# Query halves through the tail of a Mamba-2 scan block, and a new order of work at the ends of two attentions

## What is computed

```python
# layer 0: cross attention with a mask per sequence, 16 heads of 16, then LayerNorm
Q, K, V = x @ Wq.T + bq, ctx @ Wk.T + bk, ctx @ Wv.T + bv
p = softmax(where(mask == 0, -1e9, Q @ K.T / sqrt(16)))
x = layernorm((p @ V) @ Wo.T + bo + x) * ln_g + ln_b
# layer 1a: a Mamba-2 block
zxbcdt = rms(x) * norm_w @ in_proj_w            # z | xBC | dt
xh, B, C = silu(causal_conv4(xBC))
h_t = h_{t-1} * exp(dt * A) + dt * xh_t * B_t   # 8 heads of 64, state 128
u = rms((h_t . C_t + D * xh) * silu(z)) * gnorm_w
x = x + u @ out_proj_w
# layer 1b: cross attention, 8 heads of 32, mask of the keys
q = layernorm(x) @ Wq
x = x + softmax(where(pad, -1e9, q @ k.T / sqrt(32))) @ v @ Wo
```

## Time and profile before

| what | value |
|---|---|
| median of 3 runs | 8527.78 us (8526.52 to 8528.01) |
| the profiled execution | 8529.28 us |
| its span, first to last instruction | 8527.6 us |
| mean granted TensorE clock | 0.933 of full speed |
| TensorE matmul, busy | 7657.0 us, 90% |
| VectorE, busy | 5273.6 us, 62% |
| ScalarE, busy | 3407.2 us, 40% |
| GpSimd, busy | 1913.5 us, 22% |

### The profile page before, as it was taken

The page is one execution under the profiler, slowest core; times in us unless marked ns, Lnnn a source line. Parts: engine busy times, 40 slices in busy tenths (PEclk is TensorE's granted clock), DMA queues, the critical chain, the costliest instruction groups (busy, mean ns, idle before and its releaser), DMA issues.

```text
span 8527.6 us, 129102 instructions
## 1 busy us (share of the span) xinstructions
PE 7657.0 (90%) x37476; PEld 3496.5 (41%) x37796; DVE 5273.6 (62%) x12605; ACT 3407.2 (40%) x4278; POOL 1913.5 (22%) x1864
## 2 busy tenths in 40 slices
PE   3989999998998989989899899989989899898998
PEld 0353433435334353443534334343343534435343
DVE  3666565765666666666665666656666666666656
ACT  0524435343352434535244352443524345252443
POOL 3040130402203031130401304022030311304113
PEclk6989999899998989999899998999989999998999
DMA  3142230423314132231422304233141332314223
GB/s 73 28 80 38 42 68 10 80 38 51 58 23 75 30 63 55 36 55 28 77 41 37 67 15 80 38 49 60 21 77 31 59 53 34 62 30 73 45 36 63
DMA packets 230684, 422.55 MB, mean 50 GB/s; under 512 B 37209, under 2 KB 128251, under 8 KB 229769
## 3 DMA queue, kind: packets, MB, share of 16 engines
q1 hardware_dynamic: 227927, 413.21, 28.2%
q10 hardware_dynamic: 2048, 0.53, 0.0%
HBM read 191.17 MB, written 8.54 MB: 23 GB/s over the span
## 4 chain that ended last, share of the span: by engine, by line
PE 69%; DVE 12%; issue 8%; ACT 4%; DMA 3%; SPq 2%; POOL 1%; DVEq 1%; ACTq 0%; POOLq 0%
PE ps L1049 12%; PE ps L976 11%; PE ps L938 8%; PE ps L1019 7%; PE ps L1022 6%; DVE mx L1667 5%; PE ps L1024 3%; PE ps L1054 3%; ACT PR L1438 2%; PE ps L1205 2%; PE ps L996 2%; PE ps L1168 2%; PE ps L1259 1%; DVE ps L1702 1%; DMA qst<-qhl 1%
## 5 line engine op out<-in xcount | busy, mean ns | idle before, releaser
L1438 ACT ACTIVATE PR<-ps 128x1024 f32<-128x1024 f32 x2496 | 2503.4, 1024 | 2472.8 <-PE ps L1022 1247.0
L1638 DVE CUSTOM_DVE_ANT_0 ps<-ps,maskq 128x402 f32<-128x402 f32 x4203 | 2410.6, 588 | 1519.8 <-PE ps L976 1372.9
L1049 PE MATMUL ps<-PR,vbuf 128*32 128x512 f32 x9984 | 1343.2, 610 | 29.0 <-ACT PR L1438 24.0
L976 PE MATMUL ps<-kst,qst 96*128 96x402 bf16 (+1 forms) x3115 | 1017.9, 340 | 104.9 <-DVE mx L1638 73.0
L1667 DVE TENSOR_REDUCE mx<-ps 128x2 f32<-128x804 f32 x1024 | 934.1, 988 | 193.8 <-PE ps L996 192.1
L1022 PE MATMUL ps<-maskk,identb 128*128 128x512 bf16 x2592 | 984.9, 380 | 0.0
L1019 PE MATMUL ps<-qst,kst 99*128 99x512 bf16 x2496 | 916.8, 381 | 12.5 <-ACT PR L1438 5.2
L996 PE MATMUL ps<-kst,qst 100*128 100x402 f32 x2048 | 744.1, 489 | 163.6 <-DVE mx L1667 104.8
L1024 PE MATMUL ps<-qst,kst 102*128 102x512 f32 x1664 | 768.0, 526 | 100.3 <-ACT PR L1438 70.9
L976 PEld LDWEIGHTS ps<-kst,qst 96*128 96x128 bf16 x3115 | 281.8, 97 | 1194.4 <-DVE mx L1638 825.5
L756 POOL MEMSET kst<- 96x252 f32 (+1 forms) x34 | 8.7, 256 | 3023.7 <-PE ps L1049 2975.7
(11 more groups left out here) (200 smaller groups left out, 8127.0 us busy)
## 6 DMA issues: line engine op xcount, KB each, us to landing
kst<-khl SPq DMA_DIRECT2D x300, 200.1 KB, 7.5
stage<-in_maskt SPq DMA_DIRECT2D x204, 256.0 KB
stage<-in_mask SPq DMA_DIRECT2D x204, 201.0 KB
kst<-khl SPq DMA_DIRECT2D x96, 402.0 KB, 8.6
kst<-khl SPq DMA_DIRECT2D x96, 398.5 KB, 11.6
ctxs<-in_ctxt SPq DMA_DIRECT2D x17, 1601.0 KB, 17.5
qst<-q1hl SPq DMA_DIRECT2D x96, 256.0 KB
win_s<-in_w_in SPq DMA_DIRECT2D x16, 1288.0 KB, 5.8
```

The source lines that it names most:

```text
L976: pe.matmul(ps[:, bank, 0:w], QS[gi][0:KROWS, h, i * P:(i + 1) * P], KS[gi][0:KROWS, h, c0:c0 + w], start=True, stop=True).then_inc(s_raw, 1)
L1049: mm = pe.matmul(ps[32 * j:32 * j + 32, 6, :], l, PR[:, t % 2, j, :], start=(t == 0), stop=(t == KT - 1), tile_position=(0, 32 * j))
L1438: nc.scalar.activation(PR[:, t % 2, 2 * half:2 * half + 2, :], ps[:, bank:bank + 2, :], ACT.Exp, scale=scale).then_inc(s_p, 1)
L1638: nc.vector.tensor_tensor_reduce(src, src, maskq[:, i, c0:c0 + w], 1.0, -3.0e38, ALU.add, ALU.max, mx[:, c, h * QT + i:h * QT + i + 1]).th ...
```

## The change

Four edits, which touch all engines' programs.

1. *Tail by halves of 256 query rows.* `block_out(0)` and `block_out(1)` move into the scan loop's chunks 2 and 3, `rows_out(0)` to the end of chunk 2. GpSimd's inverse deviations go tile by tile. TensorE's transposes of tiles 0 and 1 stand between the last chunk's transposes and its `wout_s` products; then come the queries of the first half, the transposes of tiles 2 and 3, and the queries of the second half, each half in banks of its own. Copies and low parts go by halves, and twelve transfers of half the size replace the six. The raw pairs take the first half's rows first, head group by head group, and wait for the second half's transfers only at pair 16. TensorE waits for all four low parts before the first pair, as before.
2. *No products of constants*: `idle` is gone.
3. *End of the first attention.* `project_out` of tile 0, first three head groups, stands in front of the last group's last `times_v`, tile 1 ahead of `sums`, tile 2 ahead of `spread`, tile 3 behind it.
4. *End of the second attention.* The output projection goes to banks 4 to 7; tile 3, whose bank the spread uses, comes last as a whole. The wait for `s_fin` moves from the loop's top to behind the first step's scores, and the raw entries of the first group start at step 1 in place of 0.

```diff
-               [(FIRST1 + 48, FIRST1 + 110, 0, KT - 1)], [(FIRST1 + 110, FIRST1 + 160, 1, KT - 1)], \
+               [(FIRST1 + 48, FIRST1 + 110, 1, KT - 1)], [(FIRST1 + 110, FIRST1 + 160, 1, KT - 1)], \
...
         def raw1_place(k):
-            h, i, c = k // (QT * NC // 2), k // (NC // 2) % QT, k % (NC // 2)
+            part, k = k // (UNITS // NHALF), k % (UNITS // NHALF)
+            h, i, c = k // (HT * NC // 2), part * HT + k // (NC // 2) % HT, k % (NC // 2)
...
-        XT1_BANK = [2, 4]
+        XT1_BANK = [4, 2]
+        Q1_BANK = [[5, 7], [0, 1]]
+        NHALF = 2
+        HW = T // NHALF
+        HT = QT // NHALF
...
-            def stack_q1(b, g):
-                sp.wait_ge(s_q1, b * DT + g + 1)
+            def stack_q1(b, part, g):
+                sp.wait_ge(s_q1, (b * NHALF + part) * DT + g + 1)
                 alone(sp)
+                cols1 = slice(part * HW, (part + 1) * HW)
                 for n, (kpart, qpart) in enumerate(TERMS1):
-                    sp.dma_start(f(QS1[g][HD1 * n:HD1 * (n + 1), :, :]), f(q1hl[:, g, qpart, :])).then_inc(s_qs1[g], 16)
+                    sp.dma_start(f(QS1[g][HD1 * n:HD1 * (n + 1), :, cols1]), f(q1hl[:, g, qpart, cols1]))\
+                        .then_inc(s_qs1[g][part], 16)
...
+                if kind == "raw" and k == UNITS // NHALF:
+                    pe.wait_ge(s_qs1[g][1], LEAD + (b + 1) * STACKQ1[1])
...
+                    if gi == 0 and t == 0:
+                        pe.wait_ge(s_fin, LEAD + b * QT)
...
+                    if gi == G0 - 1 and t == KT:
+                        pe.wait_ge(s_norm, LEAD + b * NG + G0 - 1)
+                        pe.wait_ge(s_p, (b * NG + G0) * KT * 2 - 1)
+                        project_out(wo0_s, 0, G0 - 1, G0, range(1))
...
                 for g in range(G0):
                     group(b, g)
+                project_out(wo0_s, 0, G0 - 1, G0, range(1, 2))
                 sums(b, G0 - 1)
...
-                project_out(wo0_s, 0, G0 - 1, G0, range(1))
+                project_out(wo0_s, 0, G0 - 1, G0, range(2, 3))
                 spread(b, G0 - 1)
-                project_out(wo0_s, 0, G0 - 1, G0, range(1, QT))
+                project_out(wo0_s, 0, G0 - 1, G0, range(3, QT))
...
-                project_block(QT - 1)
-
-                def idle(n, bank):
...
-                idle(14, 6)
...
+                project_block(QT - 1, lambda: transposes1(0))
+                queries1(0)
                 pe.wait_ge(s_tj, (b + 1) * (QT - 1))
...
+                transposes1(1)
+                queries1(1)
...
-                pe.wait_ge(s_q1, (b + 1) * DT)
+                pe.wait_ge(s_q1, (b + 1) * DT * NHALF)
...
+                for e in LAST1:
+                    left(b + 1, e)
+                project_out(wo1_s, 0, G1 - 1, G1, range(1), 4)
                 spread(b, NG - 1)
-                project_out(wo1_s, 0, G1 - 1, G1, range(1, QT))
+                pe.wait_ge(s_ctxn, LEAD + b * NG + NG)
+                project_out(wo1_s, 0, G1 - 1, G1, range(1, QT - 1), 4)
                 pe.wait_ge(s_norm, LEAD + b * NG + NG)
-                project_out(wo1_s, G1 - 1, G1, G1)
+                project_out(wo1_s, G1 - 1, G1, G1, range(QT - 1), 4)
+                project_out(wo1_s, 0, G1, G1, range(QT - 1, QT), 4)
...
+                        if c > 1:
+                            block_out(c - 2)
                         dve.wait_ge(s_yp, LEAD + nb + 1)
...
+                            if c == 2:
+                                rows_out(0)
+
+                rows_out(1)
+                block_out(2)
+                block_out(3)
+                rows_out(2)
                 for item in LASTQ:
-                    low_q1(b, item)
+                    low_q1(b, 0, item)
+                rows_out(3)
+                for item in LASTQ:
+                    low_q1(b, 1, item)
```

More of the change, by code:

```diff
@@ L273, in xattn_mamba @@
         s_k1 = [[sem(f"s_k1_{g}_{e}") for e in range(2)] for g in range(G1)]
-        s_qs1 = [sem(f"s_qs1_{g}") for g in range(G1)]
+        s_qs1 = [[sem(f"s_qs1_{g}_{p}") for p in range(2)] for g in range(G1)]
+        s_qp1 = sem("s_qp1")
         s_r1 = sem("s_r1")
@@ L404, in xattn_mamba @@
             pj_bank[item] = 6 + n % 2
-        for n, item in enumerate(LASTQ):
-            pj_bank[item] = n % 2
         ENTRIES = []
@@ L656, in _ @@
                 rows_q1(b)
-                for g in range(G1):
-                    stack_q1(b, g)
+                for part in range(NHALF):
+                    for g in range(G1):
+                        stack_q1(b, part, g)
                 load_pieces(b, bn, PIECE1, QT * NC, False)
@@ L1082, in spread, with project_out @@
                 mm.then_inc(s_spread, 1)
+            def project_out(wo, lo, hi, n, tiles=range(QT), first=0):
+                for i in tiles:
+                    for g in range(lo, hi):
+                        mm = pe.matmul(ps[:, first + i, 0:D], ctxn[:, g, i * P:(i + 1) * P], wo[:, g, :],
+                                       start=(g == 0), stop=(g == n - 1))
+                    if hi == n:
+                        mm.then_inc(s_o, 1)
             def group(b, gi):
@@ L1150, in _ @@
                 second = list(SECOND)
-                def project_q1(item, lo, hi):
-                    i = item[2]
-                    for k in range(DT):
-                        mm = pe.matmul(ps[:, pj_bank[item], lo:hi], wq1_s[:, k, i * P:(i + 1) * P], xn[:, k, lo:hi],
-                                       start=(k == 0), stop=(k == DT - 1))
-                    return mm
                 def fill(n):
@@ L1250, in project_block @@
                     mm.then_inc(s_gt, 1)
+                    if beside_copy is not None:
+                        beside_copy()
                     pe.wait_ge(s_ut, b * QT + c + 1)
@@ L1311, in _ @@
-                idle(3, 1)
-                for i in range(QT):
-                    pe.wait_ge(s_xs1, b * QT + i + 1)
-                    for k in range(DT):
-                        mm = pe.transpose(ps[:, XT1_BANK[k], i * P:(i + 1) * P], xs1[:, i, k * P:(k + 1) * P], ident[:, :])
-                    if i >= QT - 2:
-                        mm.then_inc(s_xst1, 1)
-                    if i == QT - 2:
-                        idle(3, 1)
-                        pe.wait_ge(s_xn1, 2 * DT * b + DT)
-                        for item in LASTQ:
-                            project_q1(item, 0, i * P + P)
@@ L1323, in _ @@
-                pe.wait_ge(s_xn1, 2 * DT * (b + 1))
-                for item in LASTQ:
-                    project_q1(item, (QT - 1) * P, T).then_inc(s_proj, 1)
-                idle(14, 6)
+                transposes1(1)
+                queries1(1)
                 front = list(FRONT)
@@ L1828, in masked_windows, with block_out, rows_out @@
                                             ALU.mult).then_inc(s_M, 1)
+                def block_out(i):
+                    n = b * QT + i + 1
+                    dve.wait_ge(s_op, n)
+                    dve.wait_ge(s_gr, n)
+                    nc.vector.scalar_tensor_tensor(out=xres[:, i, :], in0=ps[:, OUT_BANK[i], 0:D], scalar=rstd[:, 2, i:i + 1],
+                                                   in1=xres[:, i, :], op0=ALU.mult, op1=ALU.add).then_inc(s_blk, 1)
+                    dve.wait_ge(s_blk, n)
+                    nc.vector.bn_stats(stats[:, i, :], xres[:, i, :]).then_inc(s_st1, 1)
+                    dve.wait_ge(s_st1, n)
+                    alone(dve)
+                    nc.vector.bn_aggr(moments[:, i, :], stats[:, i, :]).then_inc(s_mom1, 1)
+                def rows_out(i):
+                    dve.wait_ge(s_rstd1, b * QT + i + 1)
+                    dve.wait_ge(s_mom1, b * QT + i + 1)
+                    nc.vector.tensor_scalar(xs1[:, i, :], xres[:, i, :], moments[:, i, 0:1], rstd[:, 0, i:i + 1],
+                                            ALU.subtract, ALU.mult).then_inc(s_xs1, 1)
                 dve.wait_ge(s_G, b + 1)
```

107 lines of the change are left out of this document (44 added, 63 removed).

## The result

The kernel after takes 8317.3 us (median of 4 runs, 8313.7 to 8325.3), the kernel before 8527.2 (median of 4, 8522.9 to 8528.0): ratio 0.9756, 95% interval 0.9739 to 0.9773, 210 us less. Forecast were 8302 and a range of 8258 to 8385.

What follows compares the result with a forecast made beforehand. TensorE, busy 90% of 8527.6 us, was taken as the bound, so edits pay where it stands still or works ahead of something late. 16 x 10.0 + 16 x 3.7 + 15 x 0.4 = 225 us gave 8303, stated 8302; range 8258 to 8385.

Steps and rivals of the forecast that it cites:

- The tail: Last wout_s group to first raw pair: pair starts at 1054.3, not 1065.0; 10.7 us, less 0.7 for the clock: 10.0.
- first queries: Tail: query products of the first half run from 1046.0 to 1048.0, 2.0 us.
- last rows: Tail: VectorE's rows_out(3), queued behind low parts, ends at 1049.55, +3.5 us from the last wout_s group.
- second queries: Tail: query products of the second half end at 1053.1, +7.0 us from the last wout_s group.
- The transfers: Tail: halves move at 120 GB/s after 2.3 us fixed; the three needed land at 1053.8, before the low parts at 1054.2.
- The first rival: Tail: a half transfer takes as long as a whole; tail loses 1.0 us, total 8479; chance 0.15 including partial cases.
- The clock in the tail: Without constants, TensorE's gaps in the tail lower its clock: 0.7 us lost; nothing counted in the raw stage.
- the second rival: Raw stage: clock stays at half throughout, 16.8 us lost a pass including the tail's 2.2; total 8560; chance 0.03.
- The end of the first attention: Projections fill the 1.34 us hole; VectorE's first add at 1464.0, not 1467.68: 3.7 us a pass, bounds 2.5 to 4.2.
- The end of the second attention: Moved wait worth nothing; raw entries from step 1 remove a 0.48 us wait: 0.4 us, bounds -0.5 and 1.
- The scan: Scan loop: the moved block_outs, some 1.15 us each, fit VectorE's 1.93 us idle and cost nothing.
- Given back behind the raw stage: Second attention's start: GpSimd's chain ends 10.1 us earlier, so nothing is given back; 1.6 us if its waits do not close.

Runs made afterwards that it cites:

- the whole transfers: Kernel after, with six whole q1 transfers, each sent when both halves of its head group are there, in place of twelve halves: 8440.8 us, ratio 0.9901.
- the one without any: Kernel after with first group's raw entries from step 0, wait for s_fin at the loop's top and eight constant products back in the tail: 8256.2 us, ratio 0.9682.

## Why the prediction was right, step by step

- **The tail, 10.0 us a pass: 9.84.** The mechanism, no transfer left in the chain, is shown by the chain and by the whole transfers. The steps from the last `wout_s` group on came at +1.7 (first queries, forecast 2.0), +3.1 (last rows, 3.5), +6.7 (second queries, 7.0), +8.17 (first pair, 8.2).
- **The transfers, 120 GB/s for halves: cautious.** Transfers in 1041 to 1045 us, where these are nearly all that moves (it answers to the earlier trace rows):

```profile
DMA packets 624, 0.56 MB, mean 141 GB/s; under 512 B 73, under 2 KB 624, under 8 KB 624
```

  GpSimd gets the first mask piece 16.0 us behind the last `wout_s` group, not 18.0. The Trainium skill ("DMA: Bandwidth & Descriptors", section Bandwidth) has small transfers far slower than large ones, but in a table of copies from HBM; its part on small descriptors says that transfers within SBUF do not suffer so. This case agrees: 141 GB/s in transfers of 128 KB, 124 in those of 256 KB. The first rival falls with that.
- **The clock in the tail, 0.7 us: mis-sized and put in the wrong place.** It costs 1.5 us in 9 of 16 tails, 0.9 on the mean, but in the other passes it is paid in the raw stage, where I had counted nothing. Putting the constants back is worth 34 us in this kernel. Taking them out of the kernel before cost it 33 by the median, and nothing in the execution with a trace, where scan and first attention made it good. The rule that I cited for the second rival ("TensorE: Matmul & The Clock Gate", Part 1, in the Trainium skill: an array that idles falls to the lower clock) is borne out in that filling the gaps brought 2 us a pass, not as the 16.8 of that rival: from 1046 to 1050 the clock is 0.50, from 1050 to 1060 it is 0.80.
- **The end of the first attention, 3.7: 3.25, and 3.0 when it stands alone.** The hole is filled as forecast. The pass I had read was one of the 13 at the lower clock; three others, with the same gaps, ran at the full clock and had only 1.9 to give. So my reading that gaps of 1.34 and 0.72 us suffice for half speed holds for most passes, not for all. And tile 0 is 0.15 us longer than its hole.
- **The end of the second attention, +0.4: the step that failed.** That the wait's place is worth nothing was right: the jump still takes 3.5 us. The moved entries were forecast to save a wait of 0.48 us; they shortened step 0 by 1.6 us and lengthened the 12 others by 2.8. The first group lost 1.2 us a pass, and with entries from step 0 it got 1.7 back.
- **The scan, 0: +1.6, which is luck.** At a clock of 1.00 it takes 25.8 us in both kernels: the `block_out`s in it cost nothing, as forecast. The gain is the clock's. Before, the scan took 27.5 to 27.6 us at a mean clock of 0.93 to 0.94 in 15 of 16 passes; after, it did so (27.7) in one. The windows of the low stretch in the second pass before, and of a stretch at about the same place after, where the clock was 1.00 all through the scan:

```profile
1015.00:1022.00 7.00, 6.22 (x19) 3.61 (x19) 3.80 (x5) 0.72 (x2) 2.95 (x3) 0.52 1.03 157
```
```profile
1000.00:1007.00 7.00, 5.05 (x39) 4.05 (x36) 5.08 (x7) 1.21 (x3) 1.96 (x1) 1.00 1.04 123
```

  Single edits do this too: without the constants alone the kernel before has one such scan in 16, with the new end of the first attention alone five. So it follows from the edits, by way of the clock, and no term of the prediction held it. It outweighs what the first group lost.
- **Given back behind the raw stage: nothing**, as forecast. GpSimd's last khl part (row L750 at 1085.66) is 52.9 us behind the last `wout_s` group, before 62.5, and 19.98 us ahead of the attention in both.

Forecast were 14.1 us a pass, in terms of 10.0, 3.7 and 0.4; it came to 13.0, as 9.84 + 3.25 - 1.3 + 1.6 - 0.8 and 0.4 of small ones. The total is off by 15 us only because the scan's 1.6 a pass stands against the others' shortfall of some 3.

## What to carry to other kernels

Where a transfer stands in a chain, cut it so that the first consumer needs only its first half; it was the largest part of this gain. Entries spread over steps have to be weighed against the engine that takes them up: freeing one step fills the others. Count a hole before filling it, in recorded instructions, and fill it just short of its end: with constants in the raw stage, 13 more products in the last wait brought the kernel to 5 us below the one without any, 6 to 48 below.

Before a stretch is compared between two kernels, look at the same stretch in several passes: the same instructions took 7.88 or 9.5 us. And look at the stages that no edit touches: with constants in the raw stage, 1.1 us a pass of the gain was lost again in the scan.

## What the runs showed of the hardware that I had not expected

- The granted clock follows a gap at a distance: a tail with gaps of 0.97, 1.11 and 1.49 us ran at 1.00, and the pairs and the projection behind it at 0.78 and 0.50. Which of the passes pays, and where, varies from pass to pass though the gaps are the same. In the kernel after, all nine passes with a long tail had met a low stretch in the scan's first chunk: from its first product (L1300) to the last `wout_s` group they took 33.4 to 33.6 us, six of the seven with a short tail 32.1. What decides it was not settled.
- A higher mean clock need not be a shorter time: with constants in the raw stage it rose from 0.943 to 0.957 with the median within 4 us. It paid clearly only once the second attention, too, started at 1.00 (0.966, 48 us).
- The one gap of 2.25 us ahead of the second attention, with the clock at 1.00 before it, was followed by 6.8 us at 0.51. Cut to 0.28 us, with the clock of the raw stage kept up as well, it brought 48 us in 8256.
